# A fused attention and expert layer: the transposes of P·V placed between the halves of a projection

## What is computed

```python
x = x + attention(layernorm(x), Wq, Wk, Wv, Wo)
#   q, k, v = layernorm(x) @ W.T, by heads
#   attn = softmax(q k^T / 4 + bias of the causal window of 64)
#   attention = (attn v) @ Wo.T
x = x + ffn(layernorm(x), ...)
#   logits = z @ gate_w.T + lb_bias ; top 2 of 8 by sigmoid(logits)
#   each chosen expert: silu(z @ gate.T) * (z @ up.T) @ down.T, times its mean weight
#   plus the same form with the shared weights on all tokens
```

## Time and profile before

| | us |
|---|---|
| median of 3 runs | 550.24 |
| lowest and highest | 548.74, 550.45 |
| the profiled execution, device time | 550.23 |
| its span, first to last instruction | 548.4 |
| PE busy | 515.2 (94% of the span) |
| DVE busy | 392.0 (71%) |
| ACT busy | 338.1 (62%) |
| POOL busy | 228.7 (42%) |

### The profile page before, as it was taken

The page is one execution under the profiler, slowest core; times in us unless marked ns, Lnnn a source line. Parts: engine busy times, 40 slices in busy tenths (PEclk is TensorE's granted clock), DMA queues, the critical chain, the costliest instruction groups (busy, mean ns, idle before and its releaser), DMA issues.

```text
span 548.4 us, 16371 instructions
## 1 busy us (share of the span) xinstructions
PE 515.2 (94%) x5529; PEld 415.2 (76%) x5529; DVE 392.0 (71%) x1194; ACT 338.1 (62%) x776; POOL 228.7 (42%) x419
## 2 busy tenths in 40 slices
PE   6799999999999999999999678899999999999997
PEld 4567777777777777777778457788888887779996
DVE  6566788888889888878977657746666665552865
ACT  4667787887878778787777423316666666662111
POOL 5100111354245334525533536704555555554751
PEclk9999999999999999999999978979999999999999
DMA  7160101312331321221021134866455554426994
GB/s 215 62 212 5 42 4 42 91 48 88 100 99 37 102 90 39 96 102 72 26 82 62 64 138 143 266 199 213 152 159 156 151 156 131 143 90 211 398 399 159
DMA packets 42559, 69.16 MB, mean 126 GB/s; under 512 B 9708, under 2 KB 28655, under 8 KB 42480
## 3 DMA queue, kind: packets, MB, share of 16 engines
q1 hardware_dynamic: 33984, 43.46, 24.9%
q0 software_dynamic: 6480, 17.31, 8.9%
q10 hardware_dynamic: 2016, 7.34, 4.0%
HBM read 36.43 MB, written 32.06 MB: 125 GB/s over the span
## 4 chain that ended last, share of the span: by engine, by line
PE 81%; ACT 7%; DVE 5%; issue 4%; another core or an unknown queue 1%; POOL 1%; DMA 0%; SPq 0%; POOLq 0%; DVEq 0%; ACTq 0%
PE ps L571 41%; PE ps L630 8%; PE ps L660 6%; PE ps L823 5%; PE ps L914 4%; PE ps L669 3%; PE ps L625 3%; PE ps L582 3%; PE ps L646 2%; PE ps L675 2%; ACT probs L1018 2%; ACT pvs L1025 1%; PE ps L931 1%; ACT vm L991 1%
## 5 line engine op out<-in xcount | busy, mean ns | idle before, releaser
L513 POOL DMA_INDIRECT z_slots<-z,slot x64 | 64.3, 1004 | 123.7 <-PE ps L675 82.7
L571 PE MATMUL ps<-wF,wA 128*128 x639 | 105.2, 303 | 1.0 <-issue 0.4
L556 POOL DMA_INDIRECT y_rows<-vm,dest x71 | 69.6, 980 | 70.6 <-issue 41.2
L571 PEld LDWEIGHTS ps<-wF,wA 128*128 128x128 f32 x639 | 84.9, 188 | 13.9 <-issue 6.4
L1227 DVE TRANSPOSE_TENSOR_REDUCE rmax<-ps 128x32 f32<-128x1024 f32 x64 | 79.6, 1244 | 15.7 <-PE ps L630 14.0
L1018 ACT ACTIVATE probs<-ps 128x1024 f32<-128x1024 f32 x64 | 65.6, 1026 | 31.4 <-PE ps L646 30.7
L630 PE MATMUL ps<-bd,kT 64*128 64x256 f32 x512 | 66.4, 379 | 0.0
L571 PE MATMUL ps<-yT,wA 128*128 128x256 f32 x384 | 61.2, 297 | 1.5 <-DVE yT L1200 1.5
L630 PEld LDWEIGHTS ps<-bd,kT 64*128 64x128 f32 x512 | 49.9, 191 | 5.1
L571 PEld LDWEIGHTS ps<-yT,wA 128*128 128x128 f32 x384 | 49.4, 189 | 4.6 <-issue 1.9
L1125 ACT ACTIVATE vt<-ps 128x256 f32<-128x256 f32 x32 | 12.2, 384 | 58.5 <-PE ps L571 54.7
(11 more groups left out here) (202 smaller groups left out, 1106.6 us busy)
## 6 DMA issues: line engine op xcount, KB each, us to landing
z<-z_slots SPq DMA_DIRECT2D x71, 136.0 KB
zT_scratch<-zT SPq DMA_DIRECT2D x16, 512.0 KB
bd<-y_rows SPq DMA_DIRECT2D x8, 512.0 KB, 10.4
out<-xs SPq DMA_DIRECT2D x16, 256.0 KB, 7.7
wraw_of<-wffn SPq DMA_DIRECT2D x10, 384.0 KB, 4.0
xs<-x SPq DMA_DIRECT2D x7, 512.0 KB, 4.2
wA<-zT_scratch ACTq DMA_DIRECT2D x7, 512.0 KB, 6.4
z<-y_rows SPq DMA_DIRECT2D x4, 512.0 KB, 10.8
```

The costliest lines, as they stand in the source:

```text
L513: eng.indirect_dma_start(z_slots, bass.IndirectOffsetOnAxis(ap=slot[:, c, j, t:t + 1], axis=0), z[:, c, t, :], None, bounds_check=E * REGI ...
L556: eng.indirect_dma_start(y_rows, bass.IndirectOffsetOnAxis(ap=dest[:, m:m + 1], axis=0), yo[:, m, :], None, bounds_check=K * T - 1, oob_is ...
L571: mm = eng.matmul(out, lhsT(a), rhs(b), start=start and n == 0, stop=stop and n == 2, skip_group_check=skip)
```

## The change

`project` takes a second list, the halves of the contraction (`ks`), so that the second half of a projection can be issued in two parts of three products. Three conditions on the semaphores of q, k and v follow from it. In PE's `step`:

- in the first, second and third block the two transposes `pvT_of` stand behind the first three products of the projection's second half, not ahead of all six;
- in the first block the transposes of z, which stood between `pvT_of` and the six products, stand behind all of them;
- in the last block `pvT_of` stands behind `yT_of`, not ahead of it.

```diff
-                    if KT - 1 in chunks:
+                    if KT - 1 in chunks and KT - 1 in ks:
                         mm.then_inc(s_qp, 1)
...
                             maxima_T(b + 1, n2)
-                        if (old or n) and (ahead or n < 3):
-                            pvT_of(b - 1)
                         if n == 3 and ahead == 2:
                             eng.wait_ge(s_v, g + 2)
                             yT_of(g + 2)
+                        if project:
+                            project(g + 1, (1,), (0,))
+                        if (old or n) and (ahead or n < 3):
+                            pvT_of(b - 1)
+                        if project:
+                            project(g + 1, (1,), (1,))
                         if n == 0 and old >= 2:
                             zT_of(g - 2, (place - 2) % GPB)
-                        if project:
-                            project(g + 1, (1,))
                         if n == 3 and ahead and old >= 2:
                             logits_of(g - 2)
```

More of the change, by code:

```diff
@@ L617, in v_of @@
                                          lambda b: wA[:, b, 2, k, :], k == 0, k == KT - 1)
-                    if TPG - 1 in tiles:
+                    if TPG - 1 in tiles and KT - 1 in ks:
                         mm.then_inc(s_vp, 1)
```

## The result

| | before | changed |
|---|---|---|
| median, us (20 runs each) | 550.0 | 550.97 |
| lowest and highest | 546.82, 551.45 | 547.45, 554.96 |
| ratio to before, 95% interval | | 1.0044 (1.0023 to 1.0066) |
| profiled execution's span | 548.4 | 552.8 |

In these runs the changed kernel is slightly slower: by the ratio 2.4 us, by the medians 1.0. A second comparison on another occasion, 12 runs against 23, gave 0.9992 (0.9952 to 1.0032), so that the times alone don't settle even the sign. Runs of one kernel spread over 5 to 9 us, so the size has to be read where the change acts.

The account below looks back on a forecast made before the run. PE was taken to bound the kernel, busy for 515.2 of 548.4 us. Terms of -0.7, +0.1, +1.6 and 0 made +1.0 us on a median of 550.24, so 551.2 us, range 547.4 to 552.9.

Parts of the forecast that it names:

- the sum of +1.0: All groups together: -0.7, +0.1, +1.6 and 0 make the kernel 1.0 us slower.
- The chain over z's transposes: First block: later z's transposes delay ACT's copies of z, q, `oT_hi`, then `oT_lo`; second block's P·V 0.38 us later.
- 1.76 from the maxima's to o's transpose: Second block on PE: 1.76 us between these transposes in every group, with no wait.
- The signal of P·V: Second block: POOL's scatter makes P·V's signal late, fixed at about 196.87 in group 9, whatever PE does ahead.
- The rival with the signal moving along with P·V: Second block: signal 0.86 us after P·V's end, so six groups' -0.7 becomes about 0; 551.8 us, chance 0.15.
- Last block: y's transposes ahead of P·V's: o's transpose 0.11 us later, next shift 0.04 late, next first block's P·V 0.11 later.
- Six groups: Group 9 and its five like: second block gains 0.12 us each, -0.7 in all.
- Groups 7, 12, 13: Second blocks there, which waited less before: +0.1 us together.
- Groups 2, 3, 4 and 14: Second blocks there lose up to 0.47 us each, taken as 0.4: +1.6 us.
- Group 1: No transposes of z in a position that moves: 0.
- The gain of 3.4: Rival: z's chain doesn't hold P·V, second blocks of nine groups gain, 3.4 us in all; 546.8 us, chance 0.20.
- The slower rival: First block: ACT's copy of q 0.59 us behind z's, not 0.50, in thirteen groups, +1.2; 552.4 us, chance 0.22.

Follow-up runs that it names:

- the repeats: The kernel before and the changed kernel, each profiled once more: stretch from group 1 to group 15 267.70 and 268.75 us, ratios to before 0.9992 and 0.9992.
- e1: Kernel before with the new order in the first block only: stretch 269.21 us, ratio to before 1.0033.
- e4: Changed kernel with z's transposes between those of P·V and the last three products, last block in old order: stretch 264.67 us, ratio to before 0.9964.
- e7: Changed kernel with ACT's copy of q ahead of its copy of z in the first block: stretch 268.05 us, ratio to before 1.0036.
- e5: Kernel before with each group's first POOL scatter waiting for the second block's P·V: stretch 262.9 us, ratio to before 0.9898.
- e3: Kernel before with the new order in the last block only: stretch 268.60 us, ratio to before 1.0027.
- e2: Kernel before with the new order in the second and third block only: stretch 264.24 us, ratio to before 0.9945.
- e6: e2 with the scatter edit of e5: stretch 262.8 us, ratio to before 0.9906.
- e8: e4 with the scatter edit of e5: stretch 262.4 us, ratio to before 0.9892.

## Why the prediction was right where it was, point by point

The forecast was 551.2 and the median 550.97; within 0.3% had the highest chance, and the ratio, 1.0044, lies just past that bound, with the second comparison inside it. In the stretch, where it can be read, the sum of +1.0 stands against 1.35, or 1.2 with the repeats. That the median came within 0.3 of the forecast is luck in part: the ratio and the medians of the same runs differ by more than a microsecond.

**First block.** The chain over z's transposes is shown. Its terms: z's transposes ended at 193.81 in the forecast, 1.65 behind the maxima's; now 196.32 less 194.68 = 1.64. The copy of q 0.49 behind that of z, taken as 0.50 between 0.49 and 0.59. P·V at 0.64 in group 9 against 0.70, 0.76 in group 3 against 0.78. e1 shows it without the other parts, e4 takes it away. The two copies overlap by 0.10: they are 0.59 long and start 0.49 apart. The Trainium skill, ScalarE: Activation LUTs, What ACT_TABLE_LOAD costs, gives about 93 ns for back-to-back ACTIVATEs; these rows are a CAST and a COPY, and agree. What the forecast didn't see is the second path, over DVE's subtraction, 0.17 shorter than ACT's (e7); it set none of the forecast's numbers.

**Second block.** 1.76 from the maxima's to o's transpose was forecast in every group; it is 1.74 to 1.77 in groups 1 to 14. The signal of P·V was taken as fixed by the scatter, an inference. Now it is shown: in the seven profiles in which ACT waits for P·V there (both of before, e1 to e4, e7; 61 groups) the copy starts 1.42 to 1.50 behind the scatter's start, though P·V ends anywhere from 0.39 to 0.97 behind it, and e5 takes the scatter away and the wait with it. The rival with the signal moving along with P·V falls: it put the signal 0.86 behind P·V's end, and in group 9 of the changed kernel the copy starts 0.47 behind it. What is fixed is the distance from the scatter, though, not the time, as the forecast had it: the scatter itself starts 0.28 behind the shift there, in place of 0.43, and the copy 1.76, in place of 1.85. Nothing hung on that here, since the maxima's transpose is at 2.05.

**Last block.** The mechanism was right and the size off. The term is the distance from the maxima's transpose to the first one of y: 0.11 was forecast, and 0.17 it was (189.89 less 189.72), 0.16 or 0.17 in all groups. What makes it longer here, no run shows. So DVE's reciprocal and o moved by 0.17, the transpose of o is 1.61 behind the maxima's and not 1.55, and the last block took 0.10 more, not 0.04. The whole change has 1.28 in the last blocks, 0.09 each; this distance accounts for 0.06 a group more than forecast, over 12 groups 0.7, twice what is missing between 1.0 and 1.35, so something else gave a part back; what, the runs don't separate. The last blocks also cost in groups 0 and 1, which I had at nothing: 0.23 and 0.10. The 0.10 is this part's (e3 has it too). Of the 0.23, which lie ahead of the stretch and come on top of the 1.35, e3 has 0.06 and e2 0.16, so most of it comes from the other blocks' order. The 0.27 of waiting that this part was meant to fill was not removed but moved: PE now waits 0.41 for o in these blocks, where no wait of that kind was on record in groups 2 to 13.

**The sum.** Measured against forecast, in the stretch. Six groups: -0.5 against -0.7. Groups 7, 12, 13: +0.1, as forecast. Groups 2, 3, 4 and 14: +1.68 against +1.6. Group 1: +0.1 against 0.

**The rivals.** The gain of 3.4 needed P·V to stay on time. e2 shows it at 3.0 and, with e1 and e3, that the change gave it away by its other two parts. The slower rival needed copies 0.59 apart and falls with the 0.49.

## What to carry to other kernels

Work that is reordered to fill a gap has readers of its own, and so has the work that it pushes back. Here z's transposes were pushed back and had 0.06 us of slack over two other engines, and the transposes of P·V in the last block were pushed back by y's and had DVE's whole queue waiting behind them. Before filling a wait, ask why it is there: here the product had ended 0.9 us before its signal was noticed, and one changed wait on another engine took 4.4 us out of the stretch, where the best reordering alone took 3.0. And a stretch between two rows of the same line repeated within 0.4 us where 20 timed runs left anything from 1.3 to 3.6 open.

## What the runs showed of the hardware

When a product on PE ended 0.39 to 0.97 after the start of POOL's indirect scatter, ACT's copy that waited for it started only 0.3 to 0.4 us after the scatter's record ended. P·V ended at 196.01 and was noticed at 196.89; the scatter's record ran from 195.47 to 196.56. In 61 groups of seven profiles ACT's waiting copy started 1.42 to 1.50 behind the scatter's start, while P·V's own end lay 0.39 to 0.97 behind it. In e5, group 9, the maxima's transpose ended 0.16 behind the scatter's start and DVE went on 0.04 later; in e5, e6 and e8 it ended 0.01 to 0.19 behind it in groups 4 to 14 and DVE never went on more than 0.04 later. So not every signal of PE is held. Whether that is because DVE waits and not ACT, or because these ended earlier in the scatter, and whether PE's signal or ACT's notice of it is what comes late, the runs don't tell.
